# Weights and transposed activations handed over in bf16: an attention and feed-forward layer on eight cores of Trainium2

## What is computed

```python
q = (x @ Wq.T + bq).reshape(B, T, 16, 128).transpose(0, 2, 1, 3)
k = x @ Wk.T + bk                      # one head of 128 for all
v = x @ Wv.T + bv
scores = einsum('bhtd,bsd->bhts', q, k) / sqrt(128)
scores = where(pos_s < pos_t, scores, -1e30)
out = einsum('bhts,bsd->bhtd', softmax(scores), v)   # first row: 0
x = layernorm(x + out @ Wo.T + bo)

hidden = silu(x @ W1.T) * (x @ W3.T)   # W1, W3: (8192, 2048)
hidden = fwht(hidden)                  # / sqrt(8192)
x = layernorm(x + hidden @ W2.T)       # W2: (2048, 8192)
```

## Time and profile before

| | us |
|---|---|
| median of 3 runs (lowest, highest) | 5182.43 (5160.84, 5246.68) |
| the profiled execution: its device time | 5168.4 |
| its span on core 3, first to last instruction | 5166.7 |
| spans of the eight cores | 5145.2 to 5166.7 |
| busy in the span: PE, weight loads (PEld), DVE, ACT, POOL | 2953.8, 955.3, 958.3, 823.4, 149.9 |
| moved by DMA (bytes written) | 276.83 MB |
| read from HBM, written to HBM | 364.00 MB, 50.33 MB |

### The profile page before, as it was taken

The page is one execution under the profiler, slowest core; times in us unless marked ns, Lnnn a source line. Parts: engine busy times, 40 slices in busy tenths (PEclk is TensorE's granted clock), DMA queues, the critical chain, the costliest instruction groups (busy, mean ns, idle before and its releaser), DMA issues.

```text
span 5166.7 us, 30224 instructions; the slowest of 8 cores (5145.2 to 5166.7 us)
## 1 busy us (share of the span) xinstructions
PE 2953.8 (57%) x9689; PEld 955.3 (18%) x9689; DVE 958.3 (19%) x1623; ACT 823.4 (16%) x1392; POOL 149.9 (3%) x280
## 2 busy tenths in 40 slices
PE   2567434444444444444322938888888888763763
PEld 1122100000000000000000313333333333221221
DVE  0021333232222221212111150000000000003003
ACT  1111112222222222222111041111111111000000
POOL 0000000000000000000000000000000000000000
PEclk8677555555555555555555958888888988997997
DMA  9823310100000000000334223333333322333332
GB/s 138 120 44 65 90 25 14 23 12 12 12 12 12 12 4 9 12 12 0 66 69 76 59 73 58 54 52 53 53 55 52 57 49 52 111 109 99 106 109 98
DMA packets 108767, 276.83 MB, mean 54 GB/s; under 512 B 11716, under 2 KB 28228, under 8 KB 104264
## 3 DMA queue, kind: packets, MB, share of 16 engines
q0 software_dynamic: 46800, 139.48, 17.7%
q1 hardware_dynamic: 61816, 135.43, 8.1%
HBM read 364.00 MB, written 50.33 MB: 80 GB/s over the span
## 4 chain that ended last, share of the span: by engine, by line
PE 47%; DMA 17%; DVE 14%; ACT 13%; issue 7%; another core or an unknown queue 1%; DVEq 0%; ACTq 0%; SPq 0%; POOLq 0%
PE pb L180 47%; DMA W2P<-GA 9%; ACT GA L454 8%; DMA GA<-W2P 6%; DVE RR L489 2%; DVE GA L235 2%; ACT GA L231 2%; DVE pb L451 2%; DVE GA L682 2%; DVE GA L472 1%; DVE GA L475 1%; DMA GA<-X1S 1%; ACT GA L693 1%; ACT GA L679 1%
## 5 line engine op out<-in xcount | busy, mean ns | idle before, releaser
L180 PE MATMUL pb<-GA 128*128 128x512 bf16 x8576 | 2457.4, 436 | 955.0 <-ACT GA L454 649.3
L180 PEld LDWEIGHTS pb<-GA 128*128 128x128 bf16 x8576 | 842.0, 104 | 2543.5 <-issue 1858.8
L180 PE MATMUL pb<-GA,CB 64*64 64x512 bf16 (+2 forms) x824 | 435.8, 553 | 919.4 <-DVE GA L235 324.1
L454 ACT ACTIVATE GA<-pb,MNEG 128x512 bf16<-128x512 f32 x576 | 395.8, 687 | 981.5 <-PE pb L180 685.4
L180 PEld LDWEIGHTS pb<-GA,CB 64*64 64x64 bf16 (+2 forms) x824 | 87.9, 109 | 1263.0 <-issue 1261.7
L682 DVE TENSOR_TENSOR GA<-GA,pb 128x512 bf16<-128x512 f32 x128 | 88.0, 687 | 1199.8 <-PE pb L180 1076.9
L235 DVE CAST GA<-pb 64x512 bf16<-64x512 f32 x256 | 164.0, 678 | 666.7 <-DMA W2P<-GA 645.1
L231 ACT CAST GA<-pb 64x512 bf16<-64x512 f32 x256 | 135.7, 578 | 542.4 <-DMA W2P<-GA 490.8
L693 ACT ACTIVATE GA<-pb 128x512 bf16<-128x512 f32 x128 | 76.4, 597 | 596.0 <-PE pb L180 596.0
L679 ACT ACTIVATE GA<-pb 128x512 f32<-128x512 f32 x128 | 76.1, 594 | 518.1 <-PE pb L180 518.1
L469 DVE TENSOR_TENSOR GA<-GA 128x512 bf16<-128x512 bf16 x144 | 60.9, 423 | 471.6 <-ACT GA L454 471.6
(11 more groups left out here) (80 smaller groups left out, 537.3 us busy)
## 6 DMA issues: line engine op xcount, KB each, us to landing
GA<-W2P SPq DMA_DIRECT2D x256, 256.0 KB, 2.6
GA<-W2T POOLq DMA_DIRECT2D x128, 256.0 KB, 4.4
W2P<-GA SPq DMA_DIRECT2D x128, 256.0 KB, 4.9
GA<-W1S POOLq DMA_DIRECT2D x64, 512.0 KB, 5.6
GA<-W3S POOLq DMA_DIRECT2D x64, 512.0 KB, 5.4
GA<-XBT POOLq DMA_DIRECT2D x8, 2048.0 KB, 22.7
GA<-WQS POOLq DMA_DIRECT2D x4, 2048.0 KB, 15.7
GA<-XOWN SPq DMA_DIRECT2D x1, 8192.0 KB, 27.9
```

The source lines that it names most:

```text
L180: return e.matmul(out, lhsT, rhs, start=start, stop=stop, skip_group_check=True)
L454: texp = em.op("s", lambda e, qp=qp, slot=slot, g=g: e.activation(pbuf[slot], qp[:], AF.Exp, bias=MNEG[:, g:g + 1], scale=SC), waits=_mx(d ...
```

## The change

Nine inputs become bf16 in HBM: `XBT`, `XTOWN`, `WQS`, `WKS`, `WVS`, `WOS`, `W1S`, `W3S`, `W2T`. The host rounds them once with `.astype(bfloat16)`; the `dma_start` lines stay as they are and now move bf16 to bf16. The sequence of instructions on every engine is the same before and after, and so are all waits, buffers and tile sizes.

```diff
-    XBT = nc.dram_tensor("XBT", [D, T], F32, kind="ExternalInput")
-    XTOWN = nc.dram_tensor("XTOWN", [128, DC * 1024], F32, kind="ExternalInput")
+    XBT = nc.dram_tensor("XBT", [D, T], BF16, kind="ExternalInput")
+    XTOWN = nc.dram_tensor("XTOWN", [128, DC * 1024], BF16, kind="ExternalInput")
     XOWN = nc.dram_tensor("XOWN", [1024, D], F32, kind="ExternalInput")
-    WQS = nc.dram_tensor("WQS", [4, 128, 16 * 512], F32, kind="ExternalInput")
...
-    W2T = nc.dram_tensor("W2T", [HF, D], F32, kind="ExternalInput")
+    W2T = nc.dram_tensor("W2T", [HF, D], BF16, kind="ExternalInput")
...
+    bfc = ml_dtypes.bfloat16
-    WQS = C(Wq.reshape(4, 512, 16, 128).transpose(0, 3, 2, 1)).reshape(4, 128, 16 * 512)
+    WQS = C(Wq.reshape(4, 512, 16, 128).transpose(0, 3, 2, 1)).reshape(4, 128, 16 * 512).astype(bfc)
...
-    W2Tc = C(W2.T)
+    W2Tc = C(W2.T).astype(bfc)
...
-        xbT = C(xb.T)
+        xbT = C(xb.T).astype(bfc)
```

More of the change, by code:

```diff
@@ L80, in build_program @@
     nc = bass.Bass("TRN2", target_bir_lowering=False)
-    XBT = nc.dram_tensor("XBT", [D, T], F32, kind="ExternalInput")
-    XTOWN = nc.dram_tensor("XTOWN", [128, DC * 1024], F32, kind="ExternalInput")
+    XBT = nc.dram_tensor("XBT", [D, T], BF16, kind="ExternalInput")
+    XTOWN = nc.dram_tensor("XTOWN", [128, DC * 1024], BF16, kind="ExternalInput")
     XOWN = nc.dram_tensor("XOWN", [1024, D], F32, kind="ExternalInput")
-    WQS = nc.dram_tensor("WQS", [4, 128, 16 * 512], F32, kind="ExternalInput")
[L86 to L90, removed]
-    W2T = nc.dram_tensor("W2T", [HF, D], F32, kind="ExternalInput")
+    WQS = nc.dram_tensor("WQS", [4, 128, 16 * 512], BF16, kind="ExternalInput")
+    WKS = nc.dram_tensor("WKS", [128, DC * 128], BF16, kind="ExternalInput")
+    WVS = nc.dram_tensor("WVS", [128, DC * 128], BF16, kind="ExternalInput")
+    WOS = nc.dram_tensor("WOS", [4, 128, 16 * 512], BF16, kind="ExternalInput")
+    W1S = nc.dram_tensor("W1S", [64, 128, DC * 128], BF16, kind="ExternalInput")
+    W3S = nc.dram_tensor("W3S", [64, 128, DC * 128], BF16, kind="ExternalInput")
+    W2T = nc.dram_tensor("W2T", [HF, D], BF16, kind="ExternalInput")
     BQC = nc.dram_tensor("BQC", [128, 16], F32, kind="ExternalInput")
@@ L881, in _host_inputs @@
     C = np.ascontiguousarray
-    WQS = C(Wq.reshape(4, 512, 16, 128).transpose(0, 3, 2, 1)).reshape(4, 128, 16 * 512)
[L883 to L887, removed]
-    W2Tc = C(W2.T)
+    bfc = ml_dtypes.bfloat16
+    WQS = C(Wq.reshape(4, 512, 16, 128).transpose(0, 3, 2, 1)).reshape(4, 128, 16 * 512).astype(bfc)
+    WOS = C(Wo.reshape(4, 512, 16, 128).transpose(0, 3, 2, 1)).reshape(4, 128, 16 * 512).astype(bfc)
+    WKS = C(Wk.reshape(128, 16, 128).transpose(2, 1, 0)).reshape(128, 16 * 128).astype(bfc)
+    WVS = C(Wv.reshape(128, 16, 128).transpose(2, 1, 0)).reshape(128, 16 * 128).astype(bfc)
+    W1S = C(W1.reshape(64, 128, 16, 128).transpose(0, 3, 2, 1)).reshape(64, 128, 2048).astype(bfc)
+    W3S = C(W3.reshape(64, 128, 16, 128).transpose(0, 3, 2, 1)).reshape(64, 128, 2048).astype(bfc)
+    W2Tc = C(W2.T).astype(bfc)
     BQCa = C(bq.reshape(16, 128).T)
@@ L913, in _host_inputs @@
         xb = x[b]
-        xbT = C(xb.T)
+        xbT = C(xb.T).astype(bfc)
         xown = C(xb.reshape(32, 128, D)[r::4].reshape(1024, D))
-        xTown = C(xown.reshape(8, 128, 16, 128).transpose(3, 2, 0, 1)).reshape(128, 16 * 1024)
+        xTown = C(xown.reshape(8, 128, 16, 128).transpose(3, 2, 0, 1)).reshape(128, 16 * 1024).astype(bfc)
         sp = np.arange(128)[:, None]
```

## The result

The changed kernel takes 5031.8 us (median of 10 runs), the one before 5173.2 (10 runs). Executions in which one die took over 1% longer than the other at a lower granted clock are left out of every ratio here and of the times given for the experiments. The ratio is 0.974, 95% interval 0.9712 to 0.9768: 2.6% or about 135 us faster (141 by the two medians). The forecast was faster, at 5000 with a range of 4925 to 5088; the gain forecast was 170 us.

The account below looks back on a forecast made before the run. No engine alone was taken to bound the kernel; waits on DMA, mainly `W2P` stores beside loads, were the way in. Terms 26 + 35 + 8.5 + 2.5 + 34.5 + 54 + 7 + 2.6 = 170 us off 5168.4 gave 5000, range 4925 to 5088.

Parts of the forecast that it names:

- What bounds the kernel: Whole kernel: no engine alone bounds it; DMA, 17% of the chain, can act, mostly through stores the change leaves alone.
- Start: Wait before the first matmul: fewer bytes read bring it from 60.5 us to near 34, gain 26 us.
- Keys and values: Keys-and-values blocks: `XBT` lands before the store begins, stores fall from about 9.3 to 3.7 us, gain 35 us.
- The store beside the load: Attention and rest of p0: `W2P` store beside a `W2T` load falls from 4.8 to 3.7 us, gain 88.5 us.
- The meetings with large loads: Single store waits: beside first `WQS` load gain 8.5 us, second `WQS` load 2.5, two `WOS` loads 7.
- Feed-forward and down projection: Last stages: first `W1S` load gains 2.6 us; other feed-forward loads are covered by matmuls, down projection 0.
- A: Small loads: a fixed part rules, halving takes 0.6 us off, not 1.1; gain 126 us, 5042 us; chance 0.20.
- B: Stores to `W2P` don't move; only start, blocks and single waits gain, 73 us, 5095 us; chance 0.10.
- C: Stores to `W2P`: all the excess goes, each store costs 3.0 us, gain 230 us, 4938 us; chance 0.13.
- D: Whole kernel: DMA time goes by bytes written, conversion is free, time stays at 5168 us; chance 0.04.
- E: Feed-forward: PE left at a lower clock more often, +365 us at granted 0.65, 5363 us; chance 0.03.

Follow-up runs that it names:

- `W2T` alone: Only `W2T` made bf16, the other eight inputs left fp32, against the kernel before: 5099.3 us, ratio 0.981.
- X group: Only `XBT`, `XTOWN`, `WKS` and `WVS` made bf16, against the kernel before: 5136.2 us, ratio 0.988.
- large-weights run: Only `WQS`, `WOS`, `W1S` and `W3S` made bf16, against the kernel before: 5157.0 us, ratio 0.995.
- half load: Changed kernel loading only columns 0 to 1023 of each `W2T` block, later matmuls rereading them, half of `W2` left out: 4959.7 us.

## Why the prediction was right, and where its sizes were off

**What bounds the kernel, and that the stores are the way in.** Right. `W2T` alone gave 70 of 128 us, and with the load kept away from the store the store took 3.0 us in every step.

**Start.** Right: first matmul at 34.66 us where 34 was forecast, on the core that was priced. Over all cores the gain is 22.8: they started at 58.7 on average before, and at 35.9 after. The prediction's 7.1 MB ahead of the first matmul are 7.34 in the unit of its row; the sum stays at 31 us.

**Keys and values.** The mechanism was right, the size too large, 43.5 against 37.8 on the priced core (first matmul to first query matmuls: 219.6 to 181.8) and 32.4 on average. `XBT` took 13.2 us where 12 was forecast and was out of the store's way. The block period is 20.4 where 19.6 was forecast. The store takes 4.1 and not 3.7; and the 32 matmuls of a block take 9.2 to 9.3 us instead of the 8.7 seen with the X group alone on six of its cores, where the store lasts 4.8 us. These rows, core 3 of the changed kernel first and core 1 of the X-group kernel second, show it:

```profile
114.50 1.20 PE L180 MATMUL pb<-GA,CB 64*64 64x512 bf16 x2 [4.72 <-DVE GA L235]
...
115.64 9.26 PE L180 MATMUL pb<-GA 128*128 128x512 bf16 x32
```
```profile
98.59 1.20 PE L180 MATMUL pb<-GA,CB 64*64 64x512 bf16 x2 [5.07 <-DVE GA L235]
...
99.72 8.73 PE L180 MATMUL pb<-GA 128*128 128x512 bf16 x32
```

So against the X group alone about half a microsecond of the shorter wait came back as slower matmuls. Against the kernel before it is less, 9.29 against 8.97 us on average over the blocks and cores. The mean granted clock over the blocks is 0.75 in both kernels of these rows, so it does not tell why; that was not tested.

**The store beside the load.** This is the term that was mis-sized. The step "1464 / 42 / 16 = 2.2 us, halved, that is 1.1 us less" was right about the load: its engine time fell to 1.14 us. It was wrong to carry the whole of that over to the store. A store fell by 0.8 us, 4.8 to 4.0: the excess does not go one to one with the load. 30 stores in attention give 0.85 each (mean 4.87 to 4.02) and 25 us in the chain, 23.4 on average; in the rest of p0 the 48 periods between 49 stores went from 7.69 to 6.86 us, 40 us in all. I had written 34.5 and 54, and divided the same stretch by 49 periods, which gave 7.53. These two terms are 23 of the 31 us by which the priced core fell short up to the first `W1S` load.

**The meetings with large loads.** The store beside `WQS` fell to 6.38 (5.5 forecast). The one beside `WOS` fell only to 12.55, where 8.7 was forecast: gain 3, not 7. It ends with the two `WOS` loads, of which the longer takes 15.2 us. I had not taken into account that the store is issued earlier against them now, 3.4 us after the first of them and not 5.0; whether this is the reason was not tested.

**Feed-forward and down projection.** Right: worth nothing beyond the first load, as far as the scatter lets one tell, and the large-weights run shows the cover. One number of the prediction is wrong here: 134 MB is what `W1S` and `W3S` read before, and half of it, 67 MB, is what is saved. The sum does not use it.

**The rivals.** A (a fixed part, 0.6 us less a store) was nearer than I gave it credit for: the `W2T` load's own time to landing fell by just its 0.6, from 4.4 to 3.8, and the store by 0.8, between the forecast and A. The measured 5032 us lies nearer to A's 5042 than to the forecast's 5000. But its mechanism does not hold: a half load lands in 2.7 us, less than the 3.2 that were to be fixed, and the store beside it loses nearly all of its excess. The Trainium skill's form of it, "DMA: Bandwidth & Descriptors", anatomy of a DMA, a fixed 2.0 us plus bytes over 436 GB/s, gives that step of 0.6 too; its total of 2.6 us (an estimate from that page) is not what the trace has, 3.8. B (the stores don't move) and C (all excess goes) fell with the 4.0; C came true only in the kernel that keeps the load away. D fell with the `XBT` row. E (the clock) did not come as a whole, though in the profiled execution cores 4 and 5 lost 20 to 25 us each in this way. The range ends at 5088, short of B's own 5095, though the prediction says that it takes in most of B; the result did not turn on it.

## What to carry to other kernels

Before pricing fewer bytes, ask which transfer the chain waits for and what runs beside it: here 60% of the saved bytes were worth 8% of the gain, and the largest gain came through a store that the change did not touch. A load issued just ahead of a waited-for store cost that store most of the load's own engine time here from 1.1 us on, and little at 0.5; issue it behind the store, or give the store a second buffer and take it off the chain. When one wait is removed, price the change again: with the store off the chain the same bf16 inputs were worth 85 us up to the feed-forward stage instead of 128.

## What the runs showed of the hardware

A load on the software queue that converts fp32 to bf16 costs by what it reads: 256 KB read took an engine 1.20 us with conversion and 1.14 without. Rows of 1 KB in HBM did not take back what halving the bytes gave a load of 2 MB: `XBT` landed after 13.2 us instead of 22.7, though its rows halved in length too. And the queue then moved the same 139.48 MB in 34512 packets, where before the change the page counts 46800. The 12288 fewer are those of `XBT`: the trace has 16384 packets of 1 KB before and none after, and 4096 more of 4 KB. A store of 256 KB beside a load issued 0.3 us ahead of it on the other queue was delayed by 0.1 us for a load of 0.52 us of engine time and by 1.8 for one of 2.18, not in proportion in between, which I had not expected; packets and length are not separated in it.
